# Linear attention with a condition: bias sums in column groups, another bank for the last key tile, the first transfers reordered, and the last three normalisations moved to ScalarE

## What is computed

```python
xn = _ln(x, ln_w, ln_b)
q = xn @ Wq + bq
k = xn @ Wk + bk + (1.0 - src_mask) * -1000000.0
q = softmax(q.reshape(b, t, h, dh), axis=-1)      # over the 64 features of a head
k = softmax(k.reshape(b, t, h, dh), axis=1)       # over the 2048 tokens
v = ((xn @ Wv + bv) * src_mask).reshape(b, t, h, dh)
att = einsum('bnhd,bnhl->bhdl', k, v)
y = einsum('bnhd,bhdl->bnhl', q, att).reshape(b, t, d)
scale, shift = split(silu(emb) @ W_emb + b_emb, 2)
hh = _ln(y, ln2_w, ln2_b) * (1.0 + scale) + shift
return x + silu(hh) @ W_out + b_out
```

## Time and profile before

| what | value |
|---|---|
| median of three runs | 471.26 us |
| the profiled execution, its own time | 471.46 us |
| its span, first to last instruction | 469.5 us |
| TensorE busy | 459.6 us (98%) |
| TensorE weight loads busy | 375.0 us (80%) |
| VectorE / ScalarE / GpSimd busy | 347.2 / 255.7 / 133.8 us |
| chain that ended last | TensorE 97%, VectorE 1%, DMA 1% |

### The profile page before, as it was taken

One profiled execution on the slowest core, in us unless ns is written; L12 is line 12 of the kernel. 1 busy time (PEld: TensorE's weight loads), 2 busy tenths in 40 slices (PEclk: granted clock), 3 DMA queues, 4 the chain that ended last, 5 costly groups with the idle time before them and its releaser, 6 DMA issues.

```text
span 469.5 us, 7280 instructions
## 1 busy us (share of the span) xinstructions
PE 459.6 (98%) x2486; PEld 375.0 (80%) x2486; DVE 347.2 (74%) x844; ACT 255.7 (54%) x471; POOL 133.8 (28%) x149
## 2 busy tenths in 40 slices
PE   4999999999999999999999999999999999999997
PEld 3678877886888878888888888888878868888886
DVE  6768947776987947879768667676999827886852
ACT  5524322331878533347655555566799923766771
POOL 0413310221110000104323222225300032786685
PEclk9999999999999999999999999999999999999999
DMA  7936401111233201110212130312232032343322
GB/s 268 379 115 238 167 2 46 45 45 57 100 100 112 96 9 45 47 45 1 67 46 90 53 113 18 134 66 72 98 108 88 0 109 73 114 134 114 112 91 89
DMA packets 23187, 43.49 MB, mean 93 GB/s; under 512 B 1960, under 2 KB 2288, under 8 KB 23152
## 3 DMA queue, kind: packets, MB, share of 16 engines
q1 hardware_dynamic: 22592, 41.98, 26.0%
q10 hardware_dynamic: 560, 1.05, 0.6%
HBM read 34.64 MB, written 8.39 MB: 92 GB/s over the span
## 4 chain that ended last, share of the span: by engine, by line
PE 97%; DVE 1%; DMA 1%; ACT 0%; issue 0%; DVEq 0%
PE ps L1237 25%; PE ps L1239 25%; PE ps L1238 25%; PE ps L1242 10%; PE ps L1419 6%; PE ps L1341 2%; PE ps L1305 1%; PE ps L1397 1%; PE ps L1313 1%; PE ps L1262 1%; PE ps L1297 1%; DMA x_in<-in_x_dram 1%; PE ps L1401 0%; PE ps L1320 0%; ACT x_in L352 0%
## 5 line engine op out<-in xcount | busy, mean ns | idle before, releaser
L623 POOL TENSOR_TENSOR qs<-qs,qmax 128x512 f32<-128x512 f32 x32 | 36.1, 1130 | 172.0 <-DVE qmax L829 172.0
L1237 PE MATMUL ps<-wq_hi,zT_hi 128*128 128x512 f32 x128 | 52.2, 408 | 0.0
L1237 PE MATMUL ps<-wk_hi,zT_hi 128*128 128x512 f32 x124 | 51.1, 412 | 1.0 <-DVE kf L810 1.0
L338 ACT ACTIVATE zT_hi<-ps 128x512 fp32r<-128x512 f32 x32 | 19.1, 596 | 60.0 <-PE ps L1242 60.0
L1237 PE MATMUL ps<-ek_hi,zm_hi 128*128 128x512 f32 x128 | 50.4, 393 | 0.0
L1239 PE MATMUL ps<-wq_hi,zT_lo 128*128 128x512 f32 x128 | 50.2, 392 | 0.0
L1238 PE MATMUL ps<-wq_lo,zT_hi 128*128 128x512 f32 x128 | 49.9, 390 | 0.0
L1239 PE MATMUL ps<-ek_hi,zm_lo 128*128 128x512 f32 x128 | 49.9, 390 | 0.0
L1238 PE MATMUL ps<-ek_lo,zm_hi 128*128 128x512 f32 x128 | 49.8, 389 | 0.0
L1239 PE MATMUL ps<-wk_hi,zT_lo 128*128 128x512 f32 x124 | 48.7, 393 | 0.0
L1238 PE MATMUL ps<-wk_lo,zT_hi 128*128 128x512 f32 x124 | 48.3, 390 | 0.0
(11 more groups left out here) (250 smaller groups left out, 1156.8 us busy)
## 6 DMA issues: line engine op xcount, KB each, us to landing
x_in<-in_x_dram SPq DMA_DIRECT2D x35, 512.0 KB, 3.6
res<-in_x_dram SPq DMA_DIRECT2D x24, 256.0 KB, 2.8
out_dram<-res SPq DMA_DIRECT2D x24, 256.0 KB, 2.0
out_dram<-x_in SPq DMA_DIRECT2D x7, 256.0 KB, 2.0
y<-in_L_cond_Wk_dram ACTq DMA_DIRECT2D x2, 512.0 KB, 4.4
kf<-in_L_cond_Wq_dram SPq DMA_DIRECT2D x1, 1024.0 KB, 6.3
eq<-in_L_cond_W_out_dram SPq DMA_DIRECT2D x1, 1024.0 KB, 8.3
wv_mod<-in_L_cond_Wv_dram SPq DMA_DIRECT2D x1, 1024.0 KB, 10.5
```

What stands on the lines that cost most here:

```text
L338: act.activation(o, i, ACT.Copy, scale=scale).then_inc(s[done], 1)
L623: pool.tensor_tensor(q_heads, q_heads, qmax[:, n % 2, :].unsqueeze(2).broadcast_to([P, H, DH]), ALU.subtract).then_inc(s["q_shift"], 1)
L1237: pe.matmul(o, a[0], bb[0], start=start, stop=False)
```

## The change

Four edits:

1. **Bias sums in groups.** For queries and values, the four full-width matmuls become four matmuls of 32 output partitions each (`bias_parts`), one for each of the four groups, so that the four feature blocks' partial rows lie in one bank, each in 32 partitions. ScalarE copies that bank to `bias_part` (the place of the key tile `kf[15]`, not yet in use). One full matmul with `part`, a 128 by 128 tile filled with 1/32, adds the four groups up in every partition (the new `bias_sum`). The parts of the queries stand before `product_q(0, 0)`, their sum behind it; those of the values stand after tile 7, their sum after tile 8. Both sums now go to bank YB + 1.
2. **The last key tile of sequence 0** (m = 15) goes to bank OB and waits for `k_sum` 2 instead of 15. `product_g(0, 0)` waits for `k_sum` 16 before it writes the banks KB and OB.
3. **First transfers.** ScalarE's queue issues Wk's first half, `ln_w`, `ln_b`, Wk's second half.
4. **LATE = 0.** ScalarE normalises all y tiles of the last stretch.

```diff
-    LATE = 3
+    LATE = 0
...
+            load_wk(0)
             for v, at in ((ln_w, LNW), (ln_b, LNB)):
                 act.dma_start(ln_rows[at:at + NB, :], v.rearrange("(c p) -> c p", p=P)).then_inc(s["ln_in"], 16)
-            for half in range(2):
-                act.dma_start(wk_raw[:, 2 * half:2 * half + 2, :],
...
+            load_wk(1)
...
                 copy(wq_scaled[:, f, :], wq_raw[:, f, :], "wq_scaled", ln_weight(f))
+            act.wait_ge(s["bq_part"], 1)
+            copy(bias_part, ps[:, YTB, :], "bq_copy")
             normalise_x(0, 2)
             normalise_x(0, 3)
             for n in range(T):
                 if 2 <= n + 1 < T:
                     zT_high(0, n + 1)
+                if n == 8:
+                    act.wait_ge(s["bv_part"], 1)
+                    copy(bias_part, ps[:, YTB, :], "bv_copy")
...
-                dve.scalar_tensor_tensor(out=kf[:, n, :], in0=ps[:, OB if m == 1 else KB, :], scalar=pen[:, m:m + 1],
+                dve.scalar_tensor_tensor(out=kf[:, n, :], in0=ps[:, OB if m in (1, T - 1) else KB, :], scalar=pen[:, m:m + 1],
...
-            dve.tensor_tensor(bq_all[:], bq_all[:], ps[:, YTB, :], ALU.add).then_inc(s["bq_ok"], 1)
+            dve.tensor_tensor(bq_all[:], bq_all[:], ps[:, YB + 1, :], ALU.add).then_inc(s["bq_ok"], 1)
...
-                if m >= 2:
+                if m == T - 1:
+                    pe.wait_ge(s["k_sum"], 2)
+                elif m >= 2:
                     pe.wait_ge(s["k_sum"], m if m > 2 else 1)
...
-            def bias_sum(bank, by, raw, done):
+            def bias_parts(bank, by, raw, done):
 
                 for f in range(NB):
-                    last = pe.matmul(ps[:, bank, :], by[:, f:f + 1].broadcast_to([P, P]), raw[:, f, :],
-                                     start=(f == 0), stop=(f == NB - 1))
+                    last = pe.matmul(ps[32 * f:32 * f + 32, bank, :], by[:, f:f + 1].broadcast_to([P, 32]), raw[:, f, :],
+                                     start=True, stop=True)
                 last.then_inc(s[done], 1)
+
+            def bias_sum(bank, parts, done):
+                pe.matmul(ps[:, bank, :], part[:], parts, start=True, stop=True).then_inc(s[done], 1)
...
+                    if n == 0 and j in (0, 3) and b == 0:
+
+                        pe.wait_ge(s["k_sum"], T)
...
             pe.wait_ge(s["wq_in"], 16)
+            bias_parts(YTB, cols[:, LNB:LNB + NB], wq_raw, "bq_part")
             product_q(0, 0)
-            bias_sum(YTB, cols[:, LNB:LNB + NB], wq_raw, "bq_ps")
+            pe.wait_ge(s["bq_copy"], 1)
+            pe.wait_ge(s["part_ok"], 1)
+            pe.wait_ge(s["cols_ok"], 2)
+            bias_sum(YB + 1, bias_part, "bq_ps")
...
-                    pe.wait_ge(s["cols_ok"], 2)
-                    bias_sum(YB + 1, lnb_w, wv_mod, "bv_ps")
+                    bias_parts(YTB, lnb_w, wv_mod, "bv_part")
+                if n == 8:
+                    pe.wait_ge(s["bv_copy"], 1)
+                    bias_sum(YB + 1, bias_part, "bv_ps")
```

More of the change, by code:

```diff
@@ L195, in cond_linear_attention @@
         wq_scaled = eq[:, 0:4]
-        bv_all = kf[:, 14, :]
+        bias_part, bv_all = kf[:, 15, :], kf[:, 14, :]
         wemb = [eq[:, 10 + t, :] for t in range(4)] + [kf[:, 10 + t, :] for t in range(4)] + \
@@ L204, in cond_linear_attention @@
         names = """table_ok ln_in vec_in wk_in0 wk_in1 wq_in wv_in wo_in bk_in bq_in bias_in ident0 ident_ok part_ok ones_ok pick_ok
-            vec_ps cols_ok lnbw_ok kb_ps bq_ps bv_ps bk_ok bq_ok row_ok
+            vec_ps cols_ok lnbw_ok kb_ps bq_part bq_copy bq_ps bv_part bv_copy bv_ps bk_ok bq_ok row_ok
             wk_hi_ok wk_lo_ok wq_hi_ok wq_scaled wq_lo_ok wv_ok wo_hi_ok wo_lo_ok
@@ L341, in ln_weight, with load_wk @@
                 return cols[:, LNW + f:LNW + f + 1]
+            def load_wk(half):
+                act.dma_start(wk_raw[:, 2 * half:2 * half + 2, :],
+                              wk.rearrange("(c p) n -> p c n", p=P)[:, 2 * half:2 * half + 2, :]).then_inc(s[f"wk_in{half}"], 16)
+            load_wk(0)
             for v, at in ((ln_w, LNW), (ln_b, LNB)):
                 act.dma_start(ln_rows[at:at + NB, :], v.rearrange("(c p) -> c p", p=P)).then_inc(s["ln_in"], 16)
-            for half in range(2):
-                act.dma_start(wk_raw[:, 2 * half:2 * half + 2, :],
-                              wk.rearrange("(c p) n -> p c n", p=P)[:, 2 * half:2 * half + 2, :]).then_inc(s[f"wk_in{half}"], 16)
+            load_wk(1)
             def normalise_x(b, n):
@@ L1271, in product_k @@
                 for f in range(NB if m else 0):
-                    last = split_product(ps[:, OB if m == 1 else KB, :], (zT_hi[:, n % 2, f, :], zT_lo[:, n % 2, f, :]),
+                    last = split_product(ps[:, OB if m in (1, T - 1) else KB, :], (zT_hi[:, n % 2, f, :], zT_lo[:, n % 2, f, :]),
                                          (wk_hi[:, f, :], wk_lo[:, f, :]), f == 0, f == NB - 1)
```

## The result

The changed kernel takes **468.55 us** (median of six runs, 468.08 to 468.68) against 471.94 us of the kernel before on the same chip (six runs, 470.62 to 472.29): ratio 0.993 with the 95% interval 0.9917 to 0.9944, 3.4 us less. The forecast was 467.8 us, in a range of 466.2 to 469.7.

The account below looks back on a forecast made before the run. TensorE, busy for 98% of the span, was taken as the bound. Bias sums -3.3, last key tile -1.2, first transfers +1.0 and LATE 0 gave -3.5 us: 467.8 us, range 466.2 to 469.7.

Parts of the forecast that it names:

- The forecast case: Whole kernel: the four edits together bring -3.5 us, giving 467.8 us; chance 0.63.
- Bias sums: Query and value bias on TensorE: each sum falls from 3.43 to 1.79 us, 3.3 us gained for both.
- The last key tile: Last key tile's product near 109 us: TensorE's wait goes, 1.17 us gained, rounded to 1.2.
- The first transfers: Kernel start: `ln` rows land later behind Wk's first half, so the whole start is 1.0 us later (0.3 to 1.2).
- What the start waits for: Kernel start: VectorE's chain to the normalised x tile sets it, not Wk; an earlier Wk wins nothing.
- TensorE's pace: Start: the doubling from 1.2 to 2.4 GHz, at about 13.6 us, moves with the work, so 1.0 us counts in full.
- rises much later: Rival at the start: TensorE's clock rises only at 17.3 us, costing 1.3 us more; 469.1 us, chance 0.12.
- The rise fixed at 13.6: Alternative at the start: the pace change stays at 13.6 us, and 0.5 us comes back.
- LATE = 0: Last stretch: ScalarE takes three normalisations from VectorE with 0.13 us left before TensorE's load; 0 us effect.
- A start that costs nothing: Rival at the first transfers: no start cost, so -4.5 us, 466.8 us; chance 0.17.
- Narrow matmuls one after the other: Rival at the bias sums: four narrow matmuls cost 3.43 us, total +1.5 us, 472.8 us, slower; chance 0.03.
- The base: Starting time of the forecast: the profiled execution's 471.46 us, with the median of the runs 0.2 us below it.

Follow-up runs that it names:

- the start alone: Kernel before with only the new order of the first transfers: 473.07 us, ratio 1.0032.
- old transfers: Changed kernel with the first transfers in the old order (`ln` rows, then both halves of Wk): 467.59 us, ratio 0.9916 against the kernel before.
- old transfers again: Changed kernel with the first transfers in the old order, run once more beside the changed kernel on one chip: 466.93 us, ratio 0.9901 against the kernel before.
- last key tile alone: Kernel before with only the last key tile moved to the other bank: 469.93 us, ratio 0.9968.
- LATE = 0 alone: Kernel before with only LATE changed from 3 to 0: 471.94 us, ratio 1.0001.
- two of them with idle matmuls: Changed kernel with the old transfer order plus unneeded 128-column matmuls on TensorE at the start: nine, 467.34 us; two, 467.06 us.
- The changed kernel's second profile: Changed kernel run once more, nothing altered: 468.50 us, ratio 0.9929 against the kernel before.
- the `ln` rows on SyncE's queue: Changed kernel with `ln_w` and `ln_b` issued by SyncE's queue between x tiles 0 and 1: 469.88 us, ratio 0.9958 against the kernel before.
- the gap filled: Changed kernel with the old transfer order and two unneeded matmuls between key bias and first turn of x: 467.06 us, ratio 0.9908 against the kernel before.

## Why the prediction was right, step by step

- **Forecast and rivals.** The forecast case came in: sum -2.9 us in the profile for a forecast of -3.5. Of the 0.6 us between them, 0.44 are in the term of the bias sums and 0.13 in that of the first transfers.
- **Bias sums**, forecast 3.3 us, measured 2.86, just outside the stated ends of 2.9 and 3.4. This term was mis-sized. The step was to price a round of narrow matmuls at 0.93, from rows where several rounds follow each other. One round by itself took 0.99, which the ends (to 1.1) had allowed for. By themselves the pieces give 2 x (3.43 - 0.99 - 0.86) = 3.16. The remaining 0.30 lies around them. At the query bias the other work between the two turns took 9.08 - 3.43 = 5.65 us before and 7.73 - 1.85 = 5.88 now, 0.23 more; at the values it is 1.58 - 1.51 = 0.07. The chain places most of it: what follows the narrow matmuls is slower. The first pass of the query product behind them has 0.43 us (L1245 at 22.60), and it had 0.23 behind full matmuls (L1237 at 20.48 before): 0.20 of the 0.23. At the values the turn behind them has 0.59 (L1250 at 66.29) for 0.43 (L1242 at 68.94 before), of which 0.09 comes back elsewhere. Why it is slower is not tested. The steps that forecast no wait all held: ScalarE's copy and the two normalisations behind it were in time.
- **The last key tile**, forecast 1.17 us before rounding, measured 1.18 in the profile.
- **The first transfers**, forecast +1.0 us, measured +1.13 in the profile, and 1.7, 0.4 and 1.6 us by the three comparisons of runs (the start alone, the old transfers once and again). The mechanism was right in its main part: the `ln` rows landed at 5.6 to 5.7 (forecast 5.3), VectorE's copy came at 6.03 (5.7), the x tile's turn at 9.54 (9.2). What failed is the assumption that only the `ln` rows become late. The second x tile did too. By turns between the queues it would have been slowed; it was held back whole. And Wk was not at 5.2 with the `ln` rows 0.1 behind, but at 4.7 with the rows 1.0 behind. The two errors partly cancel in the landing of the `ln` rows (5.7 for 5.3), which is luck. The profile's 1.13 lies within the stated 0.3 to 1.2; two of the three comparisons of runs lie above it.
- **What the start waits for.** The forecast read from one trace that Wk is not what the start waits for. It holds for that trace. But in four of the eight profiles with the old issue time of Wk (old transfers, old transfers again, last key tile alone, LATE = 0 alone) the turn of x followed the key bias without a wait, and Wk was what the start waited for. So what the new order costs differs from execution to execution: the changed kernel turned the vector rows at 18.56 and 18.34, those eight, two of them with idle matmuls, between 16.29 and 18.20.
- **TensorE's pace.** The forecast let the rise move with the work, to 14.6, and 14.6 it is. The changed kernel's second profile had 13.9, with its key bias 0.1 us later, so the exact hit is luck. The work moved by 1.35 us at the turn of x and the pace by about 1.0, so part of the delay, 0.2 us, came back: 1.35 became 1.13. The rival "rises much later" (17.3) falls: the prediction counted its 8.0 us from the key bias and then added them to the later turn of x; from the key bias in both kernels they give 6.23 + 8.0 = 14.2, near the 14.6 seen. The rise fixed at 13.6 falls by the 14.6 here and the 16.3 with the `ln` rows on SyncE's queue. The experiments show that the cause is less simple than either: the rise comes sooner where the first work has no gap.
- **LATE = 0**, forecast 0, with 0.13 us of slack by the rows of tile 28; the rows of tiles 29 to 31 show 0.15, 0.13 and 0.15, and the edit alone measures 1.0001.
- **The other rivals.** A start that costs nothing falls by the edit alone (+1.7 us). Narrow matmuls one after the other falls: four take 0.99 us, not 3.4.
- **The base.** The measured median lies 0.75 us above the forecast 467.8. The forecast was set 0.2 us below the profiled execution's sum. The comparison's kernel before had a median of 471.94 where it had been 471.26, which is why the change measures -3.4 us in the runs and -2.8 between the two profiled executions. That -3.4 comes so near the forecast -3.5 is luck of the base; the rows give -2.9.

What stays open: why Wk's first half is there anywhere from 5.6 to 8.0 us with one and the same order of issue, and how much this adds to the spread of the runs and to the differences of up to a microsecond between kernels. No kernel was run that fixes its landing.

## What to carry to other kernels

When the first transfers are reordered, write down the time at which each is issued on every queue and read their bytes as one line through the DMA engines: here a large transfer moved ahead on one queue held up the small one behind it and the tiles of the other queue as well. Ask of a wait for data what the work behind it waits for next; here the wait for Wk was long (1.7 us), and yet an earlier Wk was worth nothing in that trace, since the statistics of x set the start. Then take a second trace of the same kernel before you build on it: in others Wk landed up to 2.5 us later and did set the start. And price a replaced group of matmuls with the work around it measured again: here 0.07 and 0.23 us were lost there, mostly in the first instruction behind the narrow matmuls.

## What the runs showed of the hardware

- **Order across queues.** Transfers on two queues were served nearly whole in the order of their issue, in the stretches shown: x tile 1 landed by 4.3 with Wk behind it (4.8 in one of eight profiles), at 5.4 behind half of Wk, and at 7.0 behind all of it. What in the chip sets this order, the rows do not tell.
- **Landing times vary.** With the old order Wk's first half, always issued at about 1.6, let the key bias begin anywhere from 5.55 to 8.02 us in eight profiles. With the new order, in three profiles, TensorE never waited for it.
- **A late arrival can help.** A gap of 0.6 us in TensorE's first work went with a fast level at 13.8 us, and the gap filled, with one at 9.9 or earlier: 3.9 us or more, from one profile of each. So a Wk that lands 0.9 us later, and leaves no gap, gave a start 0.7 us earlier (16.69 against 17.43). The Trainium skill (TensorE: Matmul & The Clock Gate, section "What's actually happening") has recent activity release the fast level, which agrees in direction; the sizes are from the rows above.
- **Four narrow matmuls side by side** in full 32-bit floats take 0.99 us where one full one takes 0.86: about 15% above the price of one, and not four times it. Their eight records all start between 21.5 and 22.0, each listed with 0.6 us, so the four groups work at the same time. The next instruction pays: 0.43 us for a pass that takes 0.23 elsewhere.
